# A graph attention kernel whose chunks of gathered rows grow from four slots to eight and whose sums move from TensorE to VectorE

## What is computed

```python
xw = (x @ W).reshape(n_nodes, H, C)                    # H = 8 heads, C = 32, 32, 16
al_s = jnp.einsum('nhc,hc->nh', xw, a_src)
al_d = jnp.einsum('nhc,hc->nh', xw, a_dst)
logits = jax.nn.leaky_relu(al_s[src] + al_d[dst], 0.2)
m = jax.lax.stop_gradient(jax.ops.segment_max(logits, dst, num_segments=n_nodes))
e = jnp.exp(logits - m[dst])
denom = jax.ops.segment_sum(e, dst, num_segments=n_nodes)
alpha = e / denom[dst]
out = jax.ops.segment_sum(alpha[:, :, None] * xw[src], dst, num_segments=n_nodes)
```

## Time and profile before

| | |
|---|---|
| median of 3 runs | 5414.55 us (5406.74 to 5415.93) |
| the profiled execution | 5453.07 us, of which span 5451.5 us |
| PE busy | 2676.4 us (49%), 13804 instructions |
| DVE busy | 2371.4 us (44%), 7341 instructions |
| ACT busy | 595.3 us (11%) |
| POOL busy | 2788.5 us (51%), 2942 instructions |
| gathers of the attention loops | 2664, 2524.4 us busy, 1473.0 us idle before them |
| read from and written to HBM | 392.07 MB and 57.21 MB |

### The profile page before, as it was taken

How to read it: one execution, slowest core, us unless ns; L and a number is a source line. 1 busy time by engine, 2 the same in 40 slices (tenths; PEclk the granted TensorE clock), 3 DMA queues, 4 the chain that set the end, 5 groups by cost and what they waited for, 6 DMA issues and landing times. The chain is left out here.

```text
span 5451.5 us, 59123 instructions
## 1 busy us (share of the span) xinstructions
PE 2676.4 (49%) x13804; PEld 1949.4 (36%) x13804; DVE 2371.4 (44%) x7341; ACT 595.3 (11%) x1968; POOL 2788.5 (51%) x2942
## 2 busy tenths in 40 slices
PE   1666774254555545546455555555543333333334
PEld 1555543133333333335333333333433323323333
DVE  5888512434444444443344444444423333333333
ACT  2222400120000000003000000000020000000001
POOL 2000021366666666662666666666446666666663
PEclk9667877567766776778666666676765555555555
DMA  2222564033333333332433333333312221221222
GB/s 62 107 95 95 235 213 182 21 84 90 92 92 90 92 89 89 93 88 41 89 90 90 91 92 90 92 88 91 70 32 48 46 48 47 46 47 48 47 46 22
DMA packets 182670, 451.06 MB, mean 83 GB/s; under 512 B 99516, under 2 KB 101378, under 8 KB 177773
## 3 DMA queue, kind: packets, MB, share of 16 engines
q0 software_dynamic: 122928, 318.15, 23.8%
q1 hardware_dynamic: 47214, 128.68, 6.4%
q10 hardware_dynamic: 12384, 2.25, 0.2%
HBM read 392.07 MB, written 57.21 MB: 82 GB/s over the span
## 5 line engine op out<-in xcount | busy, mean ns | idle before, releaser
L498 POOL DMA_INDIRECT rows_all<-gat_tab,ell_list x2664 | 2524.4, 948 | 1473.0 <-issue 859.3
L1007 PE MATMUL banks<-rows_all,ident 128*128 128x264 f32 (+1 forms) x5328 | 1864.9, 521 | 2146.2 <-PEq L121 1627.2
L1007 PEld LDWEIGHTS banks<-rows_all,ident 128*128 128x128 f32 x5328 | 1345.7, 294 | 2665.3 <-issue 2462.1
L1606 DVE TENSOR_TENSOR rows_all<-rows_all,banks 128x1024 f32<-128x1024 f32 (+1 forms) x666 | 684.8, 1042 | 136.5 <-issue 62.0
L1580 DVE COPY lrel<-m_all 128x8 f32 x666 | 129.0, 194 | 1311.0 <-issue 1115.6
L1557 DVE TENSOR_TENSOR acc<-acc,banks 128x264 f32 (+1 forms) x675 | 259.7, 385 | 700.8 <-issue 346.7
L793 ACT ACTIVATE banks<-ex_in 128x40 f32<-128x40 f32 x666 | 138.3, 208 | 3731.8 <-ACTq L121 2194.0
L1550 DVE TENSOR_TENSOR acc<-acc,banks 128x264 f32 (+1 forms) x675 | 257.3, 381 | 118.8 <-issue 113.7
L863 PE MATMUL banks<-rows_all 128*128 128x52 bf16 x4992 | 189.9, 203 | 150.5 <-PEq L121 145.6
L498 POOL DMA_INDIRECT edges<-sw_d,edge_pick x28 | 32.4, 1156 | 411.9 <-POOLq L121 399.9
L863 PEld LDWEIGHTS banks<-rows_all 128*128 128x128 bf16 x4992 | 179.1, 108 | 175.5 <-issue 173.7
(11 more groups left out here) (275 smaller groups left out, 1974.1 us busy)
## 6 DMA issues: line engine op xcount, KB each, us to landing
rows_all<-gat_tab,ell_list POOLq DMA_INDIRECT x2664
x_t<-adj_d SPq DMA_DIRECT2D x11, 3328.0 KB
y_t<-adj_d SPq DMA_DIRECT2D x11, 3328.0 KB
adj_d<-x_t SPq DMA_DIRECT2D x7, 3328.0 KB, 10.3
adj_d<-y_t SPq DMA_DIRECT2D x6, 3328.0 KB, 10.1
ell_list<-ell_d SPq DMA_DIRECT2D x222, 7.5 KB
acc<-key_d SPq DMA_DIRECT2D x1, 1664.0 KB, 6.4
acc<-vec_d SPq DMA_DIRECT2D x1, 1664.0 KB
```

Source lines behind the costliest of these rows:

```text
L498: return g.indirect_dma_start(out=dst, out_offset=None, in_=table, in_offset=bass.IndirectOffsetOnAxis(ap=idx, axis=0))
L1007: last = t.matmul(sum_ps[u % SUMS][:, 0:width], ident[:, :], rows[u][:, r * width:(r + 1) * width], start=(r == 0), stop=(r == SLOTS - 1))
L1606: v.tensor_tensor(msg, msg, exp_ps[u][:, 0:SLOTS, :].unsqueeze(3).to_broadcast([P, SLOTS, HEADS, c]), ALU.mult)\
```

## The change

A chunk has eight slots, a round three chunks, and each chunk's list is loaded by itself (`SLOTS` 8, `RING` 3, `LISTED` 1, `LAG` 1). A row buffer has a ninth slot. PE does nothing in the attention loop. For each chunk DVE weighs, waits for ACT, writes the shrunk old sums into the ninth slot, multiplies the eight slots by their weights, and makes the new sums with one `tensor_reduce` over the nine slots, straight into `acc` (`fold`). It doesn't weigh the next chunk before that. `rows_free` begins at RING - LAG = 2 and is given by ACT's first exponential. `tile_kept`, `no_sums` and PE's PSUM sums go. The exponentials' places in PSUM are 128 apart for 64.

```diff
-SLOTS = 4
+SLOTS = 8
-RING = 6
+RING = 3
-LISTED = 3
+LISTED = 1
-LAG = 3
+LAG = 1
-        rows_all = sb("rows_all", [P, RING * SLOTS * max(gat_row)])
+        rows_all = sb("rows_all", [P, RING * (SLOTS + 1) * max(gat_row)])
...
                         take(act, exp_in)
-                        s.activation(exp_ps[u], ex_in[:, :, :], ACT.Exp)
+                        s.activation(exp_ps[u], ex_in[:, :, :], ACT.Exp).then_inc(rows_free, 1)
...
-                with pe.Fori(0, rounds) as it:
-                    for u in range(RING):
-                        take(pe, msg_ready)
-                        for r in range(SLOTS):
-                            last = t.matmul(sum_ps[u % SUMS][:, 0:width], ident[:, :], rows[u][:, r * width:(r + 1) * width],
-                                            start=(r == 0), stop=(r == SLOTS - 1))
-                        last.then_inc(summed, 1)
-                        take(pe, summed)
-                        pe.sem_inc(sum_made, 1)
-                        pe.sem_inc(rows_free, 1)
...
-            for u in range(RING):
-                signal(rows_free)
+            signal(rows_free, RING - LAG)
...
                         v.tensor_copy(lrel[:, SLOTS, :], plane(m_all[:, now, :]))
+                        link(v.tensor_tensor(score[:, :, :], row_h[u][:, :, :, c], sd[:, now, :].to_broadcast([P, SLOTS, HEADS]), ALU.add))
+                        link(v.scalar_tensor_tensor(lrel[:, 0:SLOTS, :], score[:, :, :], LRELU_SLOPE, score[:, :, :], ALU.mult, ALU.max))
+                        link(v.tensor_reduce(plane(m_all[:, now, :]), lrel[:, :, :].rearrange("p r h -> p h r"), AX.X, ALU.max))
+                        v.tensor_tensor(ex_in[:, :, :], lrel[:, :, :], m_all[:, now, :].to_broadcast([P, SLOTS + 1, HEADS]), ALU.subtract)\
+                            .then_inc(exp_in, 1)
...
+                    def fold(u, tile):
+
+                        at = sums[:, bass.ds(tile, 1), :].rearrange("p a (h q) -> p (a h) q", h=HEADS)
+                        v.tensor_tensor(kept[u], at, shrink[u].unsqueeze(2).to_broadcast([P, HEADS, c + 1]), ALU.mult)
+                        msg = row_h[u][:, :, :, 0:c]
+                        link(v.tensor_tensor(msg, msg, exp_ps[u][:, 0:SLOTS, :].unsqueeze(3).to_broadcast([P, SLOTS, HEADS, c]), ALU.mult))
+                        link(v.tensor_reduce(tile_of(sums, tile), by_slot[u], AX.X, ALU.add))
...
+                    tiles = [known_tile(0)]
                     for u in range(RING):
+                        weigh(u, tiles[u])
+                        if u + 1 < RING:
+                            tiles.append(known_tile(u + 1))
                         take(dve, exp_done)
-                        if u + 1 < RING:
-                            weigh(u + 1, tiles[u + 1])
+                        fold(u, tiles[u])
```

63 lines of the change are left out of this document (7 added, 56 removed).

## The result

The changed kernel took 5440.40 us (median of 6 runs, 5428.53 to 5449.20) against 5411.89 us for the kernel before in the same measurement: a ratio of 1.0051, interval 1.0037 to 1.0064. It is half a per cent slower. The forecast was 5155 us, and the range ended at 5390. Two repetitions gave 1.0057 (1.0037 to 1.0077) and 1.0010 (1.0001 to 1.0019). In the second of them both kernels came out longer, 5463 and 5459 us; the kernel before took 5410 to 5416 us in four of the measurements of this study and 5450 to 5459 us in two, while kernels that only gather took 5323 to 5327 us beside either.

The account below looks back on a forecast made before the run. POOL's gathers were taken as the bound, held up 654 us by late buffer freeing. A layer was 1173 + 75 = 1248 us for 1331; with 12 us at the ends, 260 us less: 5414.55 to 5155 us, range 4950 to 5390.

Parts of the forecast that it names:

- What bounds the kernel: Attention layers: POOL's gathers, 1.253 us each, set the time; POOL is held up 654 us of 3992.
- the pause term: POOL's waits in the attention loop after the change: 75 us a layer, with 10 and 180 as ends.
- What holds it: Late freeing of row buffers: DVE and PE get an instruction only every 0.7 us while POOL gathers; pauses refill a store.
- the first rival: Attention loop: pauses follow gathers or loop turns, not instructions; 690 us of pauses, 5620 us in all; chance 0.11.
- Gathers: POOL in each attention layer: 936 gathers for 888, 1173 us, 60 us more a layer.
- The supply's balance: DVE's 2574 instructions a layer: 1675 come while POOL gathers, the other 900 need 64 us of pause.
- DVE's work in a chunk: Weighing, exponentials and fold: 8.0 us wide, 5.6 us in the third layer, hidden under POOL's 10.02 us.
- the third rival: DVE becomes the bound of the wide layers, its reduction taking 5.1 us; 5360 us in all; chance 0.12.
- The ends: From a layer's last gather to the reciprocal: about 12 us for 17.6; 5 us less, 1 us back for cold TensorE.
- The gate and the short lead: POOL may start chunk k after the exponent of chunk k-2: no wait, with 5 us to spare.
- the second rival: The short lead of two chunks holds POOL about 3 us at every chunk; 5975 us in all; chance 0.06.
- The sign: Whole kernel: faster by over 0.2% at 0.81, within 0.2% at 0.02, slower at 0.17.

Follow-up runs that it names:

- e9: e4 with each gather fetching 64 rows instead of 128; 5323.05 us.
- e4: The changed kernel with all attention arithmetic left out, so its 2808 gathers run alone; 5326.55 us, 0.9766 of the kernel before.
- e5: e4 plus twenty tiny DVE memsets in each chunk ahead of the buffer's release, 7020 in all; 5423.47 us.
- e13: e4 plus ten small TensorE matmuls in each chunk, which DVE awaits before the buffer's release; 5544.60 us.
- e14: e4 plus twenty semaphore increments of DVE's sequencer in each chunk ahead of the buffer's release, 7020 in all; 5469.72 us.
- e16: e4 with six chunks in a loop turn for three, on the same three buffers, 960 gathers a layer; 5432.59 us.
- e3: The kernel before with chunks of eight, rounds of three, lists of one, sums two chunks late; TensorE still sums, DVE looks ahead; 5681.64 us, 1.0417.
- e11: The changed kernel with the table load out of the loop, the look-ahead back and buffers freed at the fold's end; 5542.46 us, 1.0243 of the kernel before.
- e2: The changed kernel with the reduction over nine slots replaced by four additions; 5463.07 us, 1.0016 of the kernel before.
- e10: e4 plus two strided DVE reductions over the gathered rows in each chunk ahead of the buffer's release; 5327.48 us.
- e7: The changed kernel with chunks of four, six buffers, lists of three, three additions for the reduction, table load out of the loop; 5407.80 us, 0.9992.
- e8: e7 with DVE's look-ahead back and the buffer freed by DVE at the fold's end; 5457.55 us, 1.0078 of the kernel before.
- e6: e4 with chunks of four, six buffers and lists of three as in the kernel before, 2664 gathers; 5126.09 us, 0.9467.

## Why the prediction was wrong, point by point

**What bounds the kernel.** That POOL's gathers set the time, and that bytes don't, holds (e9). The step that failed is the pause term, 75 us a layer over 936 x 1.253 us, 225 in all. It measured 450 us, twice that. e4 shows that the term could not come out: with all arithmetic gone and next to no wait for a buffer, 2808 gathers still take 334 us over 1.253 us each. The 1.253 us were read from fifteen steps between two waits, and taken for a pace that POOL keeps once nothing holds it. Over a layer without waits a gather costs 1.372 us on the mean. By that measure 2664 x 1.372 = 3655 us of the 3990 are floor, and only 335 us could be won at all; of after's 3968 us, 2808 x 1.372 = 3852 are floor, and 116 us are left. So 144 more gathers raise the floor by 198 us (180 predicted), and what lies over it falls from 335 to 116 us, by 219; predicted was a fall from 654 to 225, by 429. The floor is a subtraction and not what these two traces show: there the gathers go at 1.25 us and nearly all the rest, 630 and 426 us, is waits for a buffer. Slow gathers without waits (e4) and quick ones with them (before, after, e5) seem to stand in for each other; why is not shown.

**What holds it.** The reading of the earlier trace rows, a supply of instructions limited to one in about 0.7 us while POOL generates gathers, with a store that pauses refill, was right in kind: in e5 starved memsets hold the buffer and POOL with it, and e5, e13 and e14 show that instructions ahead of the release cost time by their number, on DVE, TensorE and the bare sequencer. In size it was wrong. By its own balance e5 would have taken 5550 us or more, and took 5423; and it left out POOL's own share. 1173 us of gathering at 0.70 us were counted as 1675 instructions "for free", while in e4 POOL alone, with few instructions beside it, falls to 1.40 us a gather after some 172. That a gather draws on the same supply is my reading, and it stays unproven: most steps of the slow part are still 1.25 us. That the loss goes with the number of gathers, and not with rows or turns, e9 and e16 show.

The Trainium skill's rule on taken branches (Runtime: NRT & Kernel Launch, Instruction fetch mechanics) was the first rival. It gave 5620 us, and e16, with half the turns and no time won, speaks against it. The page also says that the fetch is hidden under dispatch. If the 0.7 us of the sequencers are a wait for instructions, the traces don't agree; what the 0.7 us are made of no run shows.

**Gathers.** 936 for 888: exact. Their price, where nothing else holds them, is 9% higher.

**The supply's balance.** 21 instructions a chunk of DVE and 20 of TensorE, 9100 a layer, became about 2574. 335 us over some 27300 in all are 12 ns each, and 116 less the table loads' 29 over 7700 are 11 ns; in their layers e5, e13 and e14 gave 17 to 26 ns. So the number of instructions gives the direction and the order of size, not one price: by the trace e3 has a fifth fewer instructions beside the gathers than the kernel before (8539 for 10799 in the first layer) and lies 364 us over its floor for 335. TensorE's matmuls, which the prediction let "drop out" as mere waiting, are by the count of the code two thirds of the 6530 instructions a layer that went, and moving them away was worth about 94 us (e3 to e11). The 75 us of pause a layer became 150 us over the assumed pace, or 39 us over the floor of e4.

**DVE's work in a chunk.** Predicted 8.0 us wide; the clean chunk above takes 1.21 us of weighing, 0.84 to the fold, 7.03 of folding and 0.27 behind it, 9.35 us. The multiply is 2.28 us as worked out. The reduction is near the upper bound of 5.1 us and not at 2.63: 4.36 us for 2376 elements, 1.84 ns each, and 2.32 us for 1224, against 1.13 ns an element in the earlier trace rows. The slope of a side by side reduction does not carry over to a stride of 264 elements. The Trainium skill (SBUF — State Buffer, the section on the DMA port swizzle) says that each access which crosses to a new 16-byte line pays a penalty. The 1.84 ns agree with that in direction; the page gives no figure, and no run tells the stride from the short groups of nine elements. In spite of it DVE stayed under the gathers, 10.98 us for eight, so the third rival came near in the operation (4.36 us for its 5.1) and was wrong in the mechanism, as e2 and e10 show.

**What was not priced.** The diff's removal of three exponentials ahead of the loop was counted among "under 2 us". It moved a table load into each round: 117 x 1.28 us, 29 us in the time. The trace of before had one such load in a layer. How a load reaches POOL can be seen at 2000.54 below: it holds the exponential that gives the buffer, and POOL's next gather starts 2.02 us behind the last one. The lesson is in the code and not in a row: the first user of a table was taken away.

**The ends.** Five us a layer less were forecast. After, in the first layer it is 20.6 us from the last gather's start (2456.23) to the reciprocal (2476.78), for 17.6 us in the earlier trace rows: 3 us more. When the last gather went out, DVE had been stalled 4.41 us ahead of the fold of the chunk before, and two folds followed.

**The gate and the short lead.** Two chunks of lead did not bite at every chunk; the second rival's 5975 us are far off. But the lead has no 5 us to spare either: POOL stands for a buffer at 130 steps, and e11 holds a buffer some us longer and loses 119 us.

**The sign.** In the traces the layers got 22 us shorter: 198 us for more gathers and 219 less over the floor, with the table's 29 us inside what is left. The medians say 28 us longer, 25 in the second measurement and 4 in the third, with both kernels' times moving by 20 to 45 us between measurements. I can't say more of the sign than that three measurements of three put the change 0.1 to 0.6% behind; without the table load it gains 0.4 to 0.5%.

What stays open: what the 0.7 us are made of, whether instructions that no buffer waits for cost POOL anything, how much of e3's 364 us over its floor is the short lead, why e7's third layer, with half of DVE's work in each operation, is the longest, and the 50 us of e8.

## What to carry to other kernels

Take the pace of a bound engine from a long stretch, best from a kernel in which nothing else is left, and not from the fifteen cleanest steps: the difference of 1.253 and 1.372 us made half of the 654 us of hold-up that I saw. Beside a stream of indirect gathers count the instructions that stand between a chunk's landing and its buffer's release, matmuls' weight loads and semaphore increments included. Here each cost 11 to 26 ns on the mean, but in few long stalls. Prefer few long ones; two reductions of 3.9 us in a chunk cost next to nothing while DVE kept up. When a loop's first use of a function on ScalarE is moved, look where the table load lands.

## What the hardware showed that I had not expected

- Gathers of 128 or of 64 rows, of 544 or of 1056 bytes a row, all cost 1.37 us over a whole layer (e4, e6, e9); the first 170 or so of 128 rows come every 1.25 us, the first 132 of 64 rows every 1.21.
- 7020 semaphore increments of DVE's sequencer ahead of the buffers' release cost 143 us (e14), and 702 reductions of 3.3 us in the same place cost 1 us (e10).
- Waits for buffers and slow gathers seem to take each other's place: e5 has 458 us of the first and 15 of the second, e4 5 and 326.
- A small fp32 matmul is four instructions on TensorE, 62 ns together where a buffer waits for them (e13).
- A reduction over a stride of 264 fp32 elements takes 1.84 ns an element, one over neighbours 1.13.
- A table load of 1283 ns in each of 117 rounds shows as 29 us, a fifth of its 150 us. The Trainium skill (ScalarE: Activation LUTs, What ACT_TABLE_LOAD costs) gives that same 1283 ns, and a drain of 1380 ns on top of it for every switch to a different set. Here no time for a drain shows (and no other set is seen in use between two of these loads): the exponents' input is done at 2000.42, the load starts at 2000.54 and ends at 2001.82, and the exponential starts at 2001.84:

```profile
2000.54 1.28 ACT L784 ACT_TABLE_LOAD   x1 [10.36 <-issue]
2001.84 0.23 ACT L784 ACTIVATE banks<-ex_in 128x72 f32<-128x72 f32 x1
```
